# A cleared spare tile behind 48 of GpSimd's indirect transfers in a two-layer mixture-of-experts kernel

## The reference

```python
x = layernorm(x + latent_attention(x))      # 16 heads, causal over all 1024 tokens
x = layernorm(x + experts_64(x))            # 8 of 64 experts a token, 128 places each, width 96
x = layernorm(x + recurrent(x))             # state_t = f_t * state_(t-1) + g_t, gated read-out
x = layernorm(x + experts_8(x) + shared(x)) # 2 of 8 experts a token, width 512; shared width 1024
```

## Time and profile before

| | us |
|---|---|
| median of the 3 runs | 817.85 |
| lowest and highest of the 3 | 814.3, 819.14 |
| profiled execution: span from its first to its last instruction | 851.6 |
| GpSimd busy in the profiled span | 271.2 |
| TensorE busy in the profiled span | 786.6 |

### The profile page before, as it was taken

The page is one execution under the profiler, slowest core; times in us unless marked ns, Lnnn a source line. Parts: engine busy times, 40 slices in busy tenths (PEclk is TensorE's granted clock), DMA queues, the critical chain, the costliest instruction groups (busy, mean ns, idle before and its releaser), DMA issues.

```text
span 851.6 us, 16159 instructions
## 1 busy us (share of the span) xinstructions
PE 786.6 (92%) x4635; PEld 660.7 (78%) x4635; DVE 556.9 (65%) x1423; ACT 394.8 (46%) x898; POOL 271.2 (32%) x357
## 2 busy tenths in 40 slices
PE   8998999999899999999879998899999799999957
PEld 7887877778787887777677877788897688888746
DVE  4324778877778787777345555468856387778536
ACT  1334656656565666655123343323333266666411
POOL 2004445534333232222345545524415100000241
PEclk9999999999999999999889999999999999999979
DMA  7449950000000000073176999687621335555321
GB/s 212 102 107 384 406 198 34 34 27 27 21 27 28 20 21 14 27 240 135 51 230 184 323 319 296 213 288 257 246 99 69 106 112 150 149 149 153 95 69 49
DMA packets 62881, 120.74 MB, mean 142 GB/s; under 512 B 18272, under 2 KB 32864, under 8 KB 62688
## 3 DMA queue, kind: packets, MB, share of 16 engines
q1 hardware_dynamic: 51824, 95.41, 35.2%
q0 software_dynamic: 7680, 21.51, 7.0%
q10 hardware_dynamic: 3312, 3.02, 1.0%
HBM read 76.13 MB, written 43.78 MB: 141 GB/s over the span
## 4 chain that ended last, share of the span: by engine, by line
PE 65%; DVE 11%; issue 11%; ACT 4%; POOL 3%; another core or an unknown queue 3%; DMA 2%; DVEq 0%; SPq 0%; ACTq 0%; POOLq 0%
PE scores L1627 9%; PE scores L1625 8%; PE scores L1626 8%; PE scores L1849 5%; PE acc_ps L2035 4%; PE misc_ps L1755 3%; PE probsT_ps L1762 3%; PE probsT_ps L1740 3%; PE misc_ps L1753 3%; DVE xT_lo L1096 3%; PE scores L1859 3%; PE acc_ps L1740 2%; PE probsT_ps L1979 2%; DVE neg_max L1090 2%
## 5 line engine op out<-in xcount | busy, mean ns | idle before, releaser
L826 ACT ACTIVATE area<-scores,neg_max 128x128 f32<-128x128 f32 (+7 forms) x128 | 94.9, 742 | 87.7 <-DVE neg_max L1090 85.5
L1090 DVE TENSOR_REDUCE neg_max<-scores 128x1 f32<-128x128 f32 (+7 forms) x128 | 95.8, 750 | 22.1 <-PE scores L1712 20.8
L708 POOL DMA_INDIRECT xe_d<-x_rows,send_i x64 | 64.1, 1001 | 55.5 <-ACT x_rows L850 38.5
L738 POOL DMA_INDIRECT ye_d<-area,home_i x64 | 61.4, 959 | 58.7 <-issue 28.6
L1849 PE MATMUL scores<-area 128*96 128x128 f32 x512 | 69.1, 279 | 2.1 <-issue 1.3
L1625 PE MATMUL scores<-kT_hi,weff_hi 128*128 128x512 f32 (+3 forms) x172 | 66.8, 388 | 0.9 <-ACT area L803 0.4
L1849 PEld LDWEIGHTS scores<-area 128*96 128x96 f32 x512 | 60.5, 166 | 5.2 <-issue 2.7
L1627 PE MATMUL scores<-kT_hi,weff_lo 128*128 128x512 f32 (+3 forms) x172 | 61.7, 359 | 0.0
L1626 PE MATMUL scores<-kT_lo,weff_hi 128*128 128x512 f32 (+3 forms) x172 | 61.5, 358 | 0.0
L696 POOL CAST weff_hi<-area 128x256 fp32r<-128x256 f32 x42 | 17.0, 406 | 136.5 <-PE scores L1712 88.8
L1755 PE MATMUL misc_ps<-xT_lo,xT_hi 128*128 128x512 f32 x144 | 58.4, 406 | 2.2 <-DVE xT_lo L1096 2.1
(11 more groups left out here) (290 smaller groups left out, 2081.4 us busy)
## 6 DMA issues: line engine op xcount, KB each, us to landing
area<-w SPq DMA_DIRECT2D x23, 512.0 KB, 4.0
area<-gate_up SPq DMA_DIRECT2D x24, 384.0 KB
xe_d<-area SPq DMA_DIRECT2D x8, 1088.0 KB, 11.3
ye_d<-area SPq DMA_DIRECT2D x8, 1024.0 KB, 16.7
area<-w SPq DMA_DIRECT2D x8, 1024.0 KB, 7.2
area<-ye_d SPq DMA_DIRECT2D x15, 512.0 KB, 5.2
area<-xe_d SPq DMA_DIRECT2D x28, 272.0 KB
area<-down SPq DMA_DIRECT2D x24, 192.0 KB
```

What stands on the lines that cost most here:

```text
L826: act.activation(row_of(n)[:, 0:L], score_bank(n)[:, 0:L], ACT.Exp, bias=neg_max[:, n % 4:n % 4 + 1], accum_out=rsum[:, s, k:k + 1]).then_ ...
L1090: dve.tensor_reduce(neg_max[:, n % 4:n % 4 + 1], score_bank(n)[:, 0:(n // HEADS + 1) * P], AX.X, ALU.max, negate=True).then_inc(max_ready, 1)
```

## The change

A tile `pause` of 128 x 256 f32 (128 KB, 1 KB a partition) and a semaphore `paused` are added. The new function `keep_apart` writes zeros to the tile on GpSimd, increments the semaphore when that is done, and makes GpSimd wait for it before its next instruction. It is called behind each send of tiles 6 and 7 (16 times), behind each of the 16 sends to the second experts, and behind each of the 16 final gathers: 48 times. Nobody reads the tile. The 64 transfers of `send_home` and the sends of tiles 0 to 5 stay as they were.

```diff
+        pause = sb("pause", [P, HID])
...
+        paused = sem("paused")
...
+            pauses = [0]
+
+            def keep_apart():
+
+                pauses[0] += 1
+                pool.memset(pause[:], 0.0).then_inc(paused, 1)
+                pool.wait_ge(paused, pauses[0])
+
             def send(t, k):
                 pool.wait_ge(send_done, t + 1)
                 pool.wait_ge(exp_done, t + 1)
                 pool.indirect_dma_start(xe_d, bass.IndirectOffsetOnAxis(send_i[:, t, k:k + 1], 0), x1_rows[:, t, :],
                                         None).then_inc(sent[k % 2] if t < TILES - 1 else sent_last[k], 16)
+                if t >= TILES - 2:
+                    keep_apart()
...
                 for k in range(TOP1):
                     pool.indirect_dma_start(xd_d, bass.IndirectOffsetOnAxis(slot1[:, t, k:k + 1], 0),
                                             x1[:, t, :], None).then_inc(sent1, 16)
+                    keep_apart()
...
                 for k in range(TOP1):
                     pool.indirect_dma_start(last_rows[:, t, k, :], None, yd_d,
                                             bass.IndirectOffsetOnAxis(slot1[:, t, k:k + 1], 0)).then_inc(moved[t], 16)
+                    keep_apart()
```

## The result

The changed kernel took 833.76 us (median of 4 runs, 832.27 to 837.19) against 817.58 for the kernel before (4 runs, 814.3 to 819.14): ratio 1.0212, 95% interval 1.0184 to 1.024. It is slower by 16 us where the forecast said 7. In all that follows, a run more than 1.5% above the fastest of its kernel is left out of the ratios, but not out of the medians.

What follows compares the result with a forecast made beforehand. TensorE was taken as busy for most of the span, with GpSimd fills mattering only where a transfer's landing ends a wait. Terms 0 + 0.3 + 4.5 + 2.1 = +6.9 on 817.85 gave 824.8 us; range 800 to 829.5.

Steps and rivals of the forecast that it cites:

- the two sums: Whole kernel: without late increments in plain runs +6.9, 824.8 us (chance 0.39, chosen); with them as in the profile, -18.9.
- late increments: Four GpSimd bursts: TensorE's semaphore increments get through late while GpSimd issues indirect transfers back to back; waits sum to 25.7 us.
- The test that I had named: Whole kernel: profiled span falling some 19 us while plain runs do not would mean the recording made the stalls.
- late readings: Four GpSimd bursts: TensorE's results read late in the profile, by 2.4 us at tile 6 and 4.0 at tile 7.
- Rivals 1 and 3: Plain runs: late increments real, 799 us, chance 0.28; or a third of the profile's size, 818 +- 3, chance 0.10.
- Tile 6: Sends of tile 6: eight fills add 2.4 us, hidden in GpSimd's 7.66 idle before the layer norm's power; cost 0.
- Tile 7: Sends to the first experts: one per 1.56 us against the experts' 1.53 each; 0 to 2.4, taken 0.3.
- Second experts: Sends to the second experts: 15 fills delay the first block's rows, TensorE stands still, no cover; +4.5 us.
- rival 2: Second experts and end: TensorE's 5.1 us stop lowers its clock (2.5), fills cost 0.39; about 829.5 us, chance 0.23.
- Final gathers: Last stage: last gather starts 4.5 us later, part hidden behind the shared tiles; +2.1 us (0 to 3.5).

## Why the prediction was wrong

**The choice between the two sums was right.** Ordinary runs have no late increments: before, profiled again, spans 814.1. The test that I had named came out as written, the profiled span down by 21.1 (19 forecast) and the timed runs not. That 21.1 lies so near 19 is luck: it is the 37.5 of the one long execution (851.6 against 814.1) less 16.4 that the fills cost (830.5 against 814.1), and the test, which named the recording as the cause, would have misled. My reason was half right: I put the late readings down to the recording, and every later recording is free of them, so they belong to one execution and not to recording as such. The Trainium skill's rule on recording (NOTIFIC — the notification-queue block, section 7.1) is thus neither borne out nor refuted; no run here shows that block. Rivals 1 and 3 rested on late increments and fall.

**Tile 6: right.** Cost 0; measured 1.6, not told from none. The power has 0.62 idle before it where the forecast left 5.3 of the earlier trace rows's 7.66. In the kernel that only counts and waits it has 3.10, so that is the cover in an ordinary execution, and the fills use all but 0.62 of it. Right in its size, then, but with a cover less than half of the one it was argued from.

**Tile 7: the step that failed.** "The supply goes from one in 1.26 us to one in 1.56", and for the whole term 0.3, at most 2.4. It goes to one in 2.17, because a raise of a count stands behind the fill's wait. Seven steps at 0.64 over the experts' pace of 1.53, in place of 0.03, are 4.5; the term measured 7.2 (4.7 to 9.6; 5.2 by the medians). I had listed the semaphore wait as an uncertainty of at most 0.15 a fill, and I had not walked the instructions behind the wait one by one: `sem_inc` stands in the loop. I also left out that in SP's queue the eighth row load holds all later loads back. That is about 7 of the missing 9 to 13 us.

**Second experts: the stop right, its clock not counted.** +4.5 forecast. The interval is 1.57 (0.97, 0.33 and 0.28, each rounded), in the range of 1.47 to 1.65. The stop grew from 1.29 to 5.29, so 4.0. The fourth tile went from 3.62 to 6.01 in the changed kernel, so 2.4 and a sum of 6.4; with fills at this place alone it went to 4.95, so 1.3 and a sum of 5.3, where 6.2 was measured (3.9 to 8.5; 5.2 by the medians). The clock's part is rival 2's mechanism, priced there at 2.5 for a stop of 5.1. With 0.23 it was not the forecast, yet both falls in the earlier trace rows stood behind a stop. What I held against it, a shorter stop, did not come.

**Final gathers: both parts small.** +2.1 forecast, 6.1 measured. The stop grew from 1.12 to 4.52, 3.4 in place of 2.1. From the last gather's start to TensorE's restart I had 8.6 without fills and 6.4 with them, since VectorE then waits for the landing; it was 9.1 (793.44 to 802.56) and 7.6 (809.67 to 817.31). A gather lands in 2.8 and not in the 2.1 that I took from the earlier trace rows, and 15 intervals added 5.0 and not 4.5. And the last 32 matmuls took 9.94 in place of 7.17: 2.8 that neither the sum nor rival 2 (about 1 at the end) had.

**The sum.** Tile 7 as measured alone, the rest by rows of the changed kernel: 7.2 + 6.4 + 4.1 + 1.7 (stop and clock at the end) = 19.4, against 17.3 and 19.7 measured. Rival 2 had the right sign and, but for tile 7, the right mechanism; its terms add up to 829.7, not 829.5, and with tile 7 at 7.2 in place of 0.3 to 836.6. It had fills at 0.39 for that, where they cost 0.31 (1.57 against 1.26), so part of the nearness is luck. The range ended at 829.5, since no case in it took a stretched interval into account.

## What to carry to other kernels

Price an added instruction in its own loop, with every instruction that follows it there, and not by its duration: a raise of a count behind a wait that has just ended cost 0.60 us, nearly twice the fill's own 0.33. Where a single profiled execution is far from the timed runs, take a second one before reading stalls out of it. A wait that grows on TensorE's path is to be priced with the lower clock behind it, which here added 1.1 to 2.8 us to stops of 4.5 to 5.3 us. With shorter stops it depends on the place: 1.7 behind 2.47, nothing behind 2.34 and 2.53 at the end.

## What the runs showed of the hardware

- On GpSimd, [fill, wait for it, raise a count, transfer] has 0.88 us idle before the transfer; without the raise 0.28, with the raise ahead of the fill 0.28, with a wait for the fill before, which has long ended, 0.17. One transfer behind another has 0.30.
- A fill of 256 f32 elements a partition takes 0.33 us, of 192 0.27 to 0.28, of 1 0.11 to 0.12.
- Behind a stop of 4.5 to 5.3 us the granted clock is partly at the lower of TensorE's two levels (1.2 GHz for 2.4): 16 matmuls took 4.74 to 6.01 in place of 3.62 (four traces), 32 took 8.56 to 9.94 in place of 7.17 (four traces). The length of the stop alone does not settle it: 16 matmuls took 5.31 behind 4.01 and behind 2.47, 32 took 7.17 behind 2.34 and 2.53. Matmuls in the stop, with 0.7 to 1.5 us left standing, kept it at the upper level.
- One profiled execution of the kernel before had a span 37.5 us longer than the next one, with TensorE's results read late during each burst of GpSimd transfers; in sixteen later traces this did not recur. One timed run of the kernel before took 2714.6 us, with no cause that a trace shows.
